# Projection of a triangle block: three products of high and low parts for every group of the x pass, transpositions two groups ahead

## The reference

```
gate_proj(x, Wg, bg, W, b) = sigmoid(x @ Wg + bg) * (x @ W + b)
ab1, ab2, ab3 = gate_proj(zn, ...) * mask      # three pairs: 384 columns
pp, lp, ip    = gate_proj(each, ...)           # one pair each: 128 columns
block = einsum(bikc,bkjc->bijc, pp, ab1) + einsum(bikc,bjkc->bijc, ab2, lp) + ab3 * ip
x = x + sigmoid(zn @ Wend + bend) * (layernorm(block) @ Wsum + bsum) * mask
```

## Time and profile before

| | |
|---|---|
| three runs | 1386.9, 1388.87 and 1389.89 us; median 1388.87 us |
| profiled execution | 1392.59 us; its span, first to last instruction, is 1390.9 us |
| granted TensorE clock, mean | 0.984 of full speed |
| busy share of the span | PE 96%, PEld 81%, DVE 81%, ACT 72%, POOL 63% |
| projection | from the start to about 541 us; its 12 blocks take some 42.5 us each |

### The profile page before, as it was taken

The page is one execution under the profiler, slowest core; times in us unless marked ns, Lnnn a source line. Parts: engine busy times, 40 slices in busy tenths (PEclk is TensorE's granted clock), DMA queues, the critical chain, the costliest instruction groups (busy, mean ns, idle before and its releaser), DMA issues. The chain is left out here.

```text
span 1390.9 us, 31004 instructions
## 1 busy us (share of the span) xinstructions
PE 1329.8 (96%) x9880; PEld 1131.2 (81%) x9880; DVE 1128.2 (81%) x3059; ACT 998.9 (72%) x2331; POOL 881.0 (63%) x1418
## 2 busy tenths in 40 slices
PE   6999999999999997999899999799999999999995
PEld 3887788877788777988767776699999999999995
DVE  6889878888778973887798887667888888888896
ACT  3988889888788886555477776346777776677774
POOL 3867668676686776444388887335555555555576
PEclk9999999999999998999999999799999999999998
DMA  9999999999999999888799994212222222322223
GB/s 216 241 255 262 268 237 260 266 263 250 231 254 261 262 248 307 285 287 278 194 311 329 314 324 164 90 37 62 77 77 77 77 80 79 86 76 77 77 62 91
DMA packets 357554, 267.41 MB, mean 192 GB/s; under 512 B 60465, under 2 KB 332755, under 8 KB 357395
## 3 DMA queue, kind: packets, MB, share of 16 engines
q1 hardware_dynamic: 355832, 264.76, 71.3%
q10 hardware_dynamic: 1290, 0.46, 0.2%
q0 software_dynamic: 272, 0.21, 0.1%
HBM read 171.02 MB, written 94.37 MB: 191 GB/s over the span
## 5 line engine op out<-in xcount | busy, mean ns | idle before, releaser
L1574 ACT ACTIVATE hT<-psH_d,b 128x512 f32<-128x512 f32 x288 | 197.8, 688 | 151.6 <-PE psH_d L1614 151.5
L595 POOL TENSOR_SCALAR shared<-shared,coefs_early 128x128 f32<-128x128 f32 x468 | 202.9, 454 | 90.1 <-DVE coefs_early L355 90.1
L652 PE MATMUL psZ_a<-w_all,xT_a 128*128 128x128 f32 x1728 | 230.4, 276 | 4.6 <-DVE ip_prod L732 3.4
L652 PEld LDWEIGHTS psZ_a<-w_all,xT_a 128*128 128x128 f32 x1728 | 209.8, 192 | 8.9 <-ACT xT_a L567 5.8
L652 PE MATMUL psZ_a<-w_all,xT_block 128*128 128x384 f32 x576 | 212.8, 492 | 1.3 <-DVE low_ab L721 1.3
L583 ACT ACTIVATE sig_a<-psZ_a 128x256 f32<-128x256 f32 (+1 forms) x360 | 153.4, 426 | 72.1 <-PE psZ_a L652 45.2
L1228 DVE TENSOR_SCALAR shared<-shared,coef 128x128 f32<-128x128 f32 x288 | 185.3, 703 | 1.6 <-POOL xh_b L1646 1.6
L639 PE MATMUL psT_a<-ident,shared 128*128 128x128 f32 x1152 | 185.5, 273 | 1.0 <-DVE mask L262 1.0
L639 PEld LDWEIGHTS psT_a<-ident,shared 128*128 128x128 f32 x1152 | 142.7, 142 | 47.2 <-issue 26.8
L1639 POOL TENSOR_TENSOR u_d<-u_d,gamma 128x512 f32<-128x512 f32 x71 | 91.8, 1294 | 122.9 <-ACT u_d L1557 122.5
L96 DVE BATCH_NORM_STATS2 stats_early<-shared 128x6 f32<-128x256 f32 x336 | 127.2, 422 | 32.1 <-DMA shared<-L_conv_protein_pair_dram 21.7
(11 more groups left out here) (233 smaller groups left out, 2964.7 us busy)
## 6 DMA issues: line engine op xcount, KB each, us to landing
shared<-in_x_dram SPq DMA_DIRECT2D x48, 512.0 KB, 6.3
scratch_xT<-xT_block SPq DMA_DIRECT2D x36, 512.0 KB, 5.3
shared<-scratch_xT SPq DMA_DIRECT2D x36, 512.0 KB, 5.5
scratch_x<-x_c SPq DMA_DIRECT2D x36, 512.0 KB, 4.6
shared<-scratch_x SPq DMA_DIRECT2D x36, 512.0 KB, 3.6
shared<-in_x_dram SPq DMA_DIRECT2D x48, 256.0 KB, 5.3
shared<-L_conv_protein_pair_dram SPq DMA_DIRECT2D x24, 512.0 KB, 7.5
shared<-in_L_conv_l_pair_dram SPq DMA_DIRECT2D x24, 512.0 KB, 8.9
```

The source lines that it names most:

```text
L595: return nc.gpsimd.tensor_scalar(x, x, r, b, ALU.mult, ALU.add)
L652: ins = nc.tensor.matmul(out, turned_x(G, i, t0, size)[:, j * P:j * P + P], rhs[i], start=True, stop=True)
L1574: nc.scalar.activation(hT[:, S % 2, f, :], psH[:, f, :], ACT.Gelu, bias=s["b1"][:, f:f + 1]).then_inc(gelued, 1)
```

## The change

Every group of the x pass is projected from split operands. ACT writes the transposed tiles rounded to the one-pass type (float32r) into `x_high` (`round_turned`), DVE subtracts that from the original in PSUM and writes the rest into `x_low` (`split_low`), and PE does three matmuls a tile (high by high, high by low, low by high) in place of one float32 matmul; the low by low product is left out. The weights are split once, at the start. ACT still copies the float32 tiles into `xT_block`, now after the split. Transpositions are issued two groups ahead, and normalisation four; the copies of the other passes get a ring of three. ACT's share of the normalisation is one tile in every group. In the tables, the ip statistics of the x pass and the first chain move one group earlier. The buffers of the last phase are allocated later.

```diff
--- before.py
+++ after.py
@@ -304,6 +304,14 @@
+TURN_AHEAD, NORM_AHEAD = 2, 4
+SPLIT_GROUPS = tuple(range(TPB // 2))
+
+
+def is_split(i, g):
+    return i == 0 and g in SPLIT_GROUPS
+
+
 QG = TPB // 4
@@ -325,10 +333,10 @@
 share_out(FIRST_STATS, AT_X, 4, 2, 0, range(0, TPB, 2))
-share_out(FIRST_STATS, AT_X + 3, 4, 3, 0, range(0, IP_SPLIT, 2))
+share_out(FIRST_STATS, AT_X + 2, 4, 3, 0, range(0, IP_SPLIT, 2))
 share_out(STATS_A, AT_X, 3, 2, 0, range(LP_AHEAD, TPB, 2))
-share_out(STATS_A, AT_X + 2, 2, 3, 0, range(0, IP_SPLIT, 2))
-share_out(COEFS_A, AT_X + 4, 3, EARLY, 0, range(CHAIN_STEPS))
+share_out(STATS_A, AT_X + 1, 2, 3, 0, range(0, IP_SPLIT, 2))
+share_out(COEFS_A, AT_X + 3, 3, EARLY, 0, range(CHAIN_STEPS))
 share_out(STATS_A, AT_X + 8, 2, 3, 0, range(IP_SPLIT, TPB, 2))
@@ -408,7 +416,9 @@
             return chain_coefs[chain][:, q, k:k + 1]
-        xT, xT_block = sb("xT_a", [P, 2, 4 * P]), sb("xT_block", [P, TPB * P])
+        xT, xT_block = sb("xT_a", [P, 3, 4 * P]), sb("xT_block", [P, TPB * P])
+        x_high, x_low = sb("x_high", [P, 2, 2 * P], F32R), sb("x_low", [P, 2, 2 * P], F32R)
+        wx_high, wx_low = sb("wx_high", [P, 6 * HID], F32R), sb("wx_low", [P, 6 * HID], F32R)
         sig = sb("sig_a", [P, 2, 2 * 3 * HID])
@@ -421,6 +431,7 @@
         turned, copied, projected = sem("turned"), sem("copied"), sem("projected")
+        rounded, split, wx_made = sem("rounded_a"), sem("split_a"), sem("wx_made")
         gated, multiplied = sem("gated"), sem("multiplied")
@@ -431,24 +442,34 @@
+            if G + step < 0:
+                return None
             if G + step < NG_A:
...
-            return xT_block[:, t0 * P:(t0 + size) * P] if i == 0 else xT[:, count % 2, 0:size * P]
+            return xT_block[:, t0 * P:(t0 + size) * P] if i == 0 else xT[:, count % 3, 0:size * P]
+
+        def splits(n, count):
+
+            return sum(is_split(*GROUPS_A[c % NG_A][0:2]) for c in range(count)) + len(SPLIT_GROUPS) * n
...
-            return 2 if (i == 1 and t0 < 12) or (i == 3 and t0 == TPB - 4) else 1
+            return 1
...
             return list(range(t0 + act_share(i, t0), t0 + size))
+
+        def split_group(k):
+
+            return NG_A * (k // len(SPLIT_GROUPS)) + SPLIT_GROUPS[k % len(SPLIT_GROUPS)]
@@ -540,9 +561,9 @@
-            if ahead(G, 3, last) is None:
+            if ahead(G, NORM_AHEAD, last) is None:
                 return
-            count, (i, g, t0, size) = ahead(G, 3, last)
+            count, (i, g, t0, size) = ahead(G, NORM_AHEAD, last)
             if g == 0 or (i == 3 and t0 == IP_SPLIT):
@@ -555,23 +576,39 @@
+            def round_turned(n, count, grp):
+
+                i, g, t0, size = grp
+                act.wait_ge(turned, NG_A * n + count + 1)
+                k = splits(n, count)
+                if k >= 2:
+                    act.wait_ge(projected, split_group(k - 2) + 1)
+                nc.scalar.copy(x_high[:, k % 2, :], psT[:, count % 2, 0:size * P]).then_inc(rounded, 1)
+
             def copy_turned(n, count, grp):
...
                 act.wait_ge(turned, NG_A * n + count + 1)
-
-                need(act, projected, NG_A * n + count - 1)
+                if is_split(i, g):
+                    act.wait_ge(split, splits(n, count) + 1)
+                need(act, projected, NG_A * n + count - 2)
                 if i == 0:
...
+            def take_turned(n, G, last):
+
+                now, nxt = ahead(G, TURN_AHEAD - 1, last), ahead(G, TURN_AHEAD, last)
+                if now and is_split(*now[1][0:2]):
+                    copy_turned(n, *now)
+                if nxt:
+                    (round_turned if is_split(*nxt[1][0:2]) else copy_turned)(n, *nxt)
+
             def body(n, last):
...
                     norm(act.wait_ge, op, normed_act, n, G, act_tiles, last)
-                    nxt = ahead(G, 1, last)
-                    if nxt:
-                        copy_turned(n, *nxt)
+                    take_turned(n, G, last)
                     k = PASSES[i][1]
@@ -584,9 +621,10 @@
             setup_scalar(act)
-            for G in (-3, -2, -1):
+            for G in range(-NORM_AHEAD, 0):
                 norm(act.wait_ge, op, normed_act, 0, G, act_tiles, False)
-            copy_turned(0, 0, GROUPS_A[0])
+            for G in range(-TURN_AHEAD, 0):
+                take_turned(0, G, False)
             all_blocks(body)
@@ -641,18 +679,31 @@
                 for G, (i, g, t0, size) in enumerate(GROUPS_A):
-                    nxt = ahead(G, 1, last)
+                    nxt = ahead(G, TURN_AHEAD, last)
                     if nxt:
                         turn(n, *nxt)
-                    pe.wait_ge(copied, NG_A * n + G + 1)
+                    if is_split(i, g):
+                        pe.wait_ge(split, splits(n, G) + 1)
+                        if n == 0:
+                            pe.wait_ge(wx_made, 2)
+                    else:
+                        pe.wait_ge(copied, NG_A * n + G + 1)
...
                         out = psZ[:, G % 3, j, 0:6 * HID] if i == 0 else psZ[:, G % 3, 0, j * P:j * P + P]
-                        ins = nc.tensor.matmul(out, turned_x(G, i, t0, size)[:, j * P:j * P + P], rhs[i], start=True, stop=True)
+                        if is_split(i, g):
+                            tile = slice(j * P, j * P + P)
+                            high, low = (x[:, splits(n, G) % 2, tile] for x in (x_high, x_low))
+                            nc.tensor.matmul(out, high, wx_high[:], start=True, stop=False)
+                            nc.tensor.matmul(out, high, wx_low[:], start=False, stop=False)
+                            ins = nc.tensor.matmul(out, low, wx_high[:], start=False, stop=True)
+                        else:
+                            ins = nc.tensor.matmul(out, turned_x(G, i, t0, size)[:, j * P:j * P + P], rhs[i], start=True, stop=True)
                     ins.then_inc(projected, 1)
-            turn(0, 0, GROUPS_A[0])
+            for G in range(TURN_AHEAD):
+                turn(0, G, GROUPS_A[G])
             pe.wait_ge(mask_made, 1)
@@ -701,6 +752,9 @@
+                    nxt = ahead(G, TURN_AHEAD, last)
+                    if nxt and is_split(*nxt[1][0:2]):
+                        split_low(n, *nxt)
                     dve.wait_ge(gated, NG_A * n + G + 1)
@@ -732,6 +786,15 @@
+            def split_low(n, count, grp):
+
+                k = splits(n, count)
+                dve.wait_ge(rounded, k + 1)
+                if k >= 2:
+                    dve.wait_ge(projected, split_group(k - 2) + 1)
+                v.tensor_tensor(x_low[:, k % 2, :], psT[:, count % 2, 0:2 * P], x_high[:, k % 2, :].bitcast(F32), ALU.subtract
+                                ).then_inc(split, 1)
+
             for t in range(0, CHUNKS[1][1], 2):
@@ -740,6 +803,14 @@
             setup_vector(dve)
+            w_x = s["w_all"][:, 0:6 * HID]
+            v.tensor_copy(wx_high[:], w_x).then_inc(wx_made, 1)
+            dve.wait_ge(wx_made, 1)
+            v.tensor_tensor(wx_low[:], w_x, wx_high[:].bitcast(F32), ALU.subtract).then_inc(wx_made, 1)
+            for G in range(-TURN_AHEAD, 0):
+                first = ahead(G, TURN_AHEAD, False)
+                if is_split(*first[1][0:2]):
+                    split_low(0, *first)
             for t in range(0, TPB, 2):
@@ -1810,12 +1881,8 @@
         for name, shape in (("ident", [P, P]), ("ones", [P, P]), ("w_all", [P, 6 * HID + CH]), ("ws2", [P, 2 * CH]),
-                            ("mask", [P, NBLK * TPB]), ("coef_2", [P, 2, NBLK * TPB]),
-                            ("w1", [P, 2 * FF]), ("w2", [P, NCHUNK, CH]), ("b1", [P, NCHUNK]), ("b2", [P, CH]),
-                            ("gamma", [P, CH]), ("beta", [P, CH])):
+                            ("mask", [P, NBLK * TPB]), ("coef_2", [P, 2, NBLK * TPB])):
             s[name] = ctx.enter_context(nc.sbuf_tensor(name, shape, F32))
-        for name in ("w1_high", "w1_low"):
-            s[name] = ctx.enter_context(nc.sbuf_tensor(name, [P, 2 * FF], F32R))
         s["x2_loaded"] = [ctx.enter_context(nc.semaphore(f"loaded_d_{k}")) for k in range(len(CHUNKS))]
@@ -1832,6 +1899,10 @@
             mix_phase(nc, d, s)
+        for name, shape, kind in (("w1", [P, 2 * FF], F32), ("w2", [P, NCHUNK, CH], F32), ("b1", [P, NCHUNK], F32),
+                                  ("b2", [P, CH], F32), ("gamma", [P, CH], F32), ("beta", [P, CH], F32),
+                                  ("w1_high", [P, 2 * FF], F32R), ("w1_low", [P, 2 * FF], F32R)):
+            s[name] = ctx.enter_context(nc.sbuf_tensor(name, shape, kind))
         ffn_phase(nc, d, s)
```

## The result

| | before | changed |
|---|---|---|
| median of four runs each | 1389.27 us (1386.9 to 1389.89) | 1409.38 us (1408.27 to 1415.29) |
| profiled execution, its span | 1392.59, 1390.9 us | 1415.29, 1413.5 us |
| granted clock, mean, in that execution | 0.984 | 0.979 |

The changed kernel takes 1.0149 times as long, with an interval of 1.0129 to 1.0169: 20 us more. The forecast was 1415 us, likeliest from 1401 to 1424. The profiled execution of before is a fifth one, beside its four; that of the changed kernel is the slowest of its four.

What follows compares the result with a forecast made beforehand. PE was taken to set the pace before, DVE the changed x pass: 11 x (1.5 + 0.4) + 5.1 = 26 us more gives 1418.6 for the profiled execution, so 1415 us for the median; likeliest 1401 to 1424, 8-in-10 range 1399 to 1433.

Steps and rivals of the forecast that it cites:

- DVE sets the changed x pass: x pass: with the added splits DVE has 20.2 us of work against PE's 16.7, so the pass goes at DVE's pace.
- PE's own gain: x groups on PE: 1.39 us in place of 1.51, 0.12 us a group, some 17 us in 144 groups if PE stays the bound.
- The x pass: x pass of each block after block 0: +1.5 us from ten splits of 0.33 us on DVE; bounds +0.5 and +2.3.
- the low bound of this term: x pass: DVE's work for x10 and x11 partly done under pp0 and pp1, giving back up to 1 us: +0.5.
- The entry: Start of the x pass: x0 waits for its split and ACT's copy behind DVE's lp statistics; +0.4 us a block, 0.3 to 1.8.
- joints in the x pass: Between passes: transposing ahead would close 0.6 us a block; counted in the bounds only, since DVE holds the pass.
- The waits for loads: DVE's waits for pp and lp should mostly go: loads issued 1.33 us earlier, x pass 1.5 us longer, longest wait 2.0.
- rival 2: Entry to the x pass: waits for loads stay, the entry costs its full 1.8 us a block; 1431 to 1440 us, chance 0.15.
- Start and block 0: Weight splits, first two groups' splits and block 0's ten splits on DVE: 1.0 + 0.8 + 3.3 = +5.1 us (3 to 6).
- ACT's loop: x groups on ACT: sigmoid, norm and two copies take 1.33 us, hidden under DVE's 1.65 us.
- the chain of rounding, split, copy and the next but one transposition: x groups: dependence on the group two before takes 2.8 us for two groups, 1.4 a group, so hidden too.
- Rival 1: x pass: PE stays the bound, DVE's backlog is carried into the other passes; 22 us less, 1367 us, chance 0.09.

Runs made afterwards that it cites:

- e4: The kernel before plus, on DVE, a 256-column subtraction where each split would stand, into a buffer nobody reads or waits for: 1.0081 against before.
- e3: The changed kernel with two products a tile on PE in place of three (high by low left out): 1.0082 against before.
- e6: The changed kernel without DVE's subtraction: the third product reads the high part, PE and the copy wait for the rounding only: 0.9995 against before.
- e10: The changed kernel with rings of three for x_high and x_low, nothing else: 1.0143 against before.
- e5: The changed kernel with only the six odd x groups split: 1.0012 against before.
- e1: The changed kernel with no group split; earlier transpositions and normalisation, larger ring, moved tables and weight splits stay: 0.9977 against before.
- e2: The changed kernel with one of DVE's two products in each x group left out from block 1 on: 1404.99 us, one run.
- e11: The changed kernel with only odd x groups split, low parts made by POOL from xT_block, rings of three, ACT copies right behind the rounding: 0.9985 against before.
- e9: e6 with rings of three for x_high, the low part still left out: 1382.69 us, one run.
- e12: e11 with x11 unsplit too, so POOL splits groups 1, 3, 5, 7 and 9: 0.998 against before.
- e8: e5 with all lp statistics moved into ip2 to ip5, none in the x pass: 1.0135 against before.

## Why the prediction came out right, and where its steps did not

**DVE sets the changed x pass: right in the main.** DVE's work alone, with nothing waiting for it, gives three quarters of the x pass's loss and about half of the kernel's (e4); 0.35 us less PE work a group leaves the spacing as it was in seven of the twelve steps (x2 to x6, x9 and x10, e3); and without DVE's subtraction and the waits for it the loss is gone (e6, 0.9995). DVE's instruction did step by 0.33 us, and the six matmuls take 1.14 us in sequence (1.15 forecast). PE's whole group, at 1.31 us without a pause, came out 0.08 under the forecast: PE's own gain was put too low, which the result didn't feel. As forecast, the groups from x1 on start 1.57 to 2.26 us apart and 1.50 behind x7, in medians. Two things that the sum had left out also hold the pass. The ring of two costs 0.55 us of it (e10), and most of what e3 gains ahead of the tail lies at the same steps. And e5's miss shows that it matters where a split stands in DVE's queue, not only how much DVE has to do.

**The x pass was put a little too high:** +1.5 forecast, +1.2 measured. Two errors of opposite sign are in that, so its closeness is in part luck. DVE's work in the windows grew from 16.86 to 19.16 us, by 2.3 and not 3.3. The pass holds seven DVE instructions more (62 for 55), not ten, since its last products and statistics slip over into pp0 and pp1; DVE's busy time in the other three passes went from 19.47 to 20.39. That was the low bound of this term (+0.5). Against it, the forecast let DVE work without a gap (20.2 us), and it stood idle for 0.77 of 19.93 us. With rings of three (e10) the pass is 19.46 us: the chain through the ring, which the sum had put at nothing, is worth 0.55.

**The entry, +0.4 forecast, +0.14 on average,** is the sum of two things which I had not separated. Against e1, which has the same lead and no split, the other three passes are 24.50 - 23.42 = 1.08 us longer. That is the entry behind the split, for with x0 unsplit they take 23.46 (e5), though there a part of the delay stands in the x pass instead (2.01 us from x0 to x1, for 1.27); it is inside the 0.3 to 1.8 that I had for it but well above the 0.4 taken. The lead gives back 24.36 - 23.42 = 0.94. That the two nearly cancel was not forecast, and is luck too. I had looked for joints in the x pass only (0.6 us, left to the bounds). There the lead closes none (18.79 in e1); it takes 0.48 us out of the other three (23.76 to 23.28), which PE still holds, and the rest of the 0.94 is that fewer of them run long. The waits for loads fell as forecast, but not to nothing, and rival 2 did come true in five of the changed kernel's eleven entries. In each of them DVE waited 0.28 to 0.90 us for a load of lp ahead of the split, and PE then waited 1.37 to 1.98 us for ACT's copy; these are the five in which the other three passes take 24.8 to 25.4 us and not 24.0 to 24.2. The longest, before block 6:

```profile
293.39 0.76 DVE L96 BATCH_NORM_STATS2 stats_early<-shared 128x6 f32<-128x256 f32 x2 [0.90 <-DMA shared<-in_L_conv_l_pair_dram]
...
295.07 0.41 PE L677 MATMUL psT_a<-ident,shared 128*128 128x128 f32 x2 [1.98 <-ACT xT_block L598]
```

**Start and block 0: +6.1 us in the profiled execution, +5.1 forecast.** The start was right: 23.30 - 21.37 = 1.93 us against 1.8. The x pass of block 0 took 4.17 more (25.60 for 21.43) instead of 3.3. DVE is busy for 24.82 of its 25.60 us there. The moved table, which I had costed at nothing, puts eight statistics in one iteration; without any split it cost 1.9 us in e1.

In the profile the sum is thus 11 x (1.20 + 0.14) + 6.1 = 20.8 us to the end of the last x pass (517.71 to 538.55). The spans differ by 1.8 us more, and this lies behind that point, in the last block's other passes and the phases that the change doesn't touch. That stretch takes 868 to 876 us in the fourteen profiled executions, e1's being the shortest, so a few us between two single executions say nothing. The forecast had 26; 1415 was some 6 us above the median.

**The step that failed is the chain through the ring of two.** I had put ACT's loop at 1.33 us and the chain of rounding, split, copy and the next but one transposition at 1.4 us a group, both hidden under DVE's 1.65. The chain is 1.55: I had counted its own instructions, but not the sigmoid and the norm (0.38 and 0.39 us in sequence) that are queued on ACT between the rounding and the copy. For the changed kernel that made a small difference: 1.55 is below 1.65, but not below the pace of the groups in which DVE has less to do, and there the ring costs the 0.55 us of e10. For the question what would come if DVE were relieved it was decisive: I expected 17 us for an x pass that came out at 18.8 (e6) and 19.25 (e2). Rival 1, 22 us faster, would have failed even with its condition met, for with no subtraction at all the kernel is level with before (e6).

**Under the second limit there may be a third.** e1 and e11 take 18.8 + 23.3 = 42.1 us in their better blocks, and average 42.5. In e9 and e12 the same sum would be 17.3 + 23.5 = 40.8 and 18.3 + 23.3 = 41.6; they average 42.3 and 42.6. Where the x pass gets shorter than that, the waits for loads come back (for pp and lp together 31.8 us before, 9.2 changed, 18.5 in e1, 37.1 in e9, 32.9 in e12) and the other passes get longer. Between 45 and 535 us these four move 259 to 261 GB/s at a DMA share of 1.05 or 1.06, before 256 at 1.07, the changed kernel 246 at 1.02. That the transfers set a limit of about 42 us a block is argued from these rows and not shown; no run was made that moves fewer bytes.

The Trainium skill (TensorE: Matmul & The Clock Gate, Back-to-back issue gap) has a formula for the isolated gap that would give 162.5 ns for each of these matmuls and, as the prediction estimated from it, a group of 1.22 us. The trace has 0.17 to 0.18 us and, where PE doesn't pause, 1.31; the prediction's own 1.39 missed this by as much on the other side.

## What to carry to other kernels

A faster form on the engine that sets the pace pays only as far as the next engine allows, and here the split gave 3.3 us more to do (2.3 of it inside the pass, as it turned out) to an engine that had 1.85 us of room there: add that up before anything else. The sum is not enough, though: look also at what stands in the queue ahead of the instruction that others wait for, as with the four statistics of x1. When such a chain runs over several engines and a ring of two, count what is queued on each engine between its links, not the links alone. And when a part of a kernel is made shorter, look at whether waits for loads come back in the part beside it.

## What the runs showed of the hardware

**One-pass matmuls.** With 384 columns they start every 0.17 to 0.18 us; the first behind float32 transpositions takes 0.26 (122.29 to 122.55). So the time scales with the columns, against 0.24 at 512. The rounding of 128 x 256 on ACT takes 374 ns and a plain copy of the same size 372, so the conversion costs next to nothing (385 and 365 in e9). POOL's subtraction of 128 x 256 takes 728 ns, DVE's 416, or 0.33 in sequence.

**The clock when PE pauses.** In the first block of the changed kernel the same matmuls start 0.32 us apart at two places, little more than half the rate elsewhere (0.17 to 0.18), which goes with 1.2 GHz in place of 2.4. One is from 23.3 to 27.4, the timeline of PE:

```profile
24.09 0.52 PE L700 MATMUL psZ_a<-wx_high,x_low 128*128 128x384 f32 x1
24.41 0.52 PE L698 MATMUL psZ_a<-wx_high,x_high 128*128 128x384 f32 x1
```

The other is around 31 to 34, where the windows also show a lower granted clock, 0.72 here and 0.50 from 32 to 34:

```profile
core 0: us, PE busy (x) PEld busy (x) DVE busy (x) ACT busy (x) POOL busy (x), PEclk, DMA share, GB/s
20.00:23.00 3.00, 0.24 (x3) 0.04 (x1) 2.27 (x6) 0.74 (x3) 2.67 (x6) 1.00 1.18 256
23.00:28.00 5.00, 4.77 (x16) 4.32 (x16) 4.84 (x15) 3.19 (x7) 0.00 (x0) 1.00 1.18 240
28.00:30.00 2.00, 0.17 (x3) 0.20 (x3) 2.00 (x7) 0.91 (x4) 0.00 (x0) 1.00 1.19 226
30.00:32.00 2.00, 1.53 (x8) 1.02 (x7) 2.00 (x7) 1.10 (x4) 0.00 (x0) 0.72 1.19 208
```

Both times PE had been nearly idle before, for 0.24 of 3 us and for 0.17 of 2. In the first stretch the record says 1.00 while the matmuls start 0.32 us apart, so the interval between starts is the safer witness; why they differ stays open. Neither stretch cost time: PE was done at 27.8 and DVE's split came at 28.81; the second time PE was done at 34.6 and DVE's eight statistics at 34.9. In the steady x passes, where PE pauses for at most 0.81 us at a time, the granted clock stayed at 1.00, and so it did behind the waits of up to 1.98 us at the entries. In e3, with more idle time in every group, it did not: it was 0.50 from 167 to 169 us in block 3, behind a wait of PE of 1.20 us, and the same happened in five more of its x passes. In e8 the five x passes with a clock of 0.92 take 22.0 to 22.7 us and the six at 1.00 take 19.9 to 20.8; how much of that is the clock and how much the wait before it was not separated. The prediction had named such a fall as what would push the time up; in the changed kernel it stayed out of the steady blocks.
